# A rotary embedding's sin multiplication moved from VectorE to GpSimd, with six rotation buffers in place of three

## The reference, cut to what matters

```python
def _rotate_half(x):
    x1, x2 = (x[..., :R // 2], x[..., R // 2:])      # R = 64
    return jnp.concatenate([-x2, x1], axis=-1)

def _apply_rope(x, cos, sin):
    return x * c + _rotate_half(x) * s

kv_d = _lin(x, Wkv_d, bkv_d); q_d = _lin(x, Wq_d, bq_d)
k1 = _lin(kv_d, Wk_u, bk_u); kr = _apply_rope(_lin(x, Wrk, brk), cos, sin)
q1 = _lin(q_d, Wq_u, bq_u);  qr = _apply_rope(_lin(q_d, Wrq, brq), cos, sin)
k = jnp.concatenate([k1, kr], axis=-1); q = jnp.concatenate([q1, qr], axis=-1)
attn = softmax(q @ k / sqrt(D)); out = attn @ v; x = x + layernorm(out @ Wo + bo)
# then 16 experts, top 4 of them weighted, and a last layer norm
```

## Time and profile before

| what | us |
|---|---|
| runs shown | 8006.28 and 8179.35, median 8092.81 |
| the profiled execution, its own time | 8001.64 |
| its span on the slowest core (core 5) | 8000.1 |
| TensorE busy over the span | 6745.4 (84%) |
| VectorE busy over the span | 3149.2 (39%) |
| GpSimd busy over the span | 305.4 (4%) |

### The profile page before, as it was taken

One profiled execution on the slowest core, in us unless ns is written; L12 is line 12 of the kernel. 1 busy time (PEld: TensorE's weight loads), 2 busy tenths in 40 slices (PEclk: granted clock), 3 DMA queues, 4 the chain that ended last, 5 costly groups with the idle time before them and its releaser, 6 DMA issues.

```text
span 8000.1 us, 84460 instructions; the slowest of 8 cores (7974.1 to 8000.1 us)
## 1 busy us (share of the span) xinstructions
PE 6745.4 (84%) x31216; PEld 3081.5 (39%) x31216; DVE 3149.2 (39%) x5145; ACT 764.0 (10%) x1123; POOL 305.4 (4%) x563
## 2 busy tenths in 40 slices
PE   5444366666467999999999999999999999999995
PEld 2212122223243444444444444444444444444443
DVE  4333333334365343433434334343433434334344
ACT  2000033323010000000000000000000000000000
POOL 0111000000000000000000000000000000000000
PEclk9666566666677999999999999999999999999997
DMA  5111100000424333334334333334434334433334
GB/s 117 29 34 31 35 16 9 12 12 10 107 85 85 74 74 74 77 71 79 72 73 81 74 76 74 74 74 74 78 71 79 74 72 78 77 75 74 74 74 137
DMA packets 126286, 533.56 MB, mean 67 GB/s; under 512 B 34481, under 2 KB 59314, under 8 KB 67778
## 3 DMA queue, kind: packets, MB, share of 16 engines
q0 software_dynamic: 93184, 433.20, 29.2%
q1 hardware_dynamic: 32706, 94.96, 3.3%
HBM read 908.76 MB, written 37.75 MB: 118 GB/s over the span
## 4 chain that ended last, share of the span: by engine, by line
PE 77%; DVE 11%; DMA 6%; issue 4%; ACT 1%; DVEq 0%; another core or an unknown queue 0%; SPq 0%; ACTq 0%; POOL 0%; POOLq 0%
PE psum L1075 23%; PE psum L1030 22%; PE psum L1036 22%; DMA rotb<-krs 4%; PE psum L634 2%; PE psum L693 2%; DVE probsT L678 2%; PE psum L672 1%; PE psum L619 1%; DVE krs L462 1%; PE psum L425 1%; PE psum L891 1%; DVE stat L644 1%; DVE stat L829 1%; DVE stat L378 1%
## 5 line engine op out<-in xcount | busy, mean ns | idle before, releaser
L1030 PE MATMUL psum<-tT,w1sl 128*128 128x512 bf16 x8192 | 1854.7, 380 | 0.0
L1036 PE MATMUL psum<-tT,w1sl 128*128 128x512 bf16 x8192 | 1852.0, 380 | 0.0
L1075 PE MATMUL psum<-act_e,w2sl 128*128 128x512 bf16 x8192 | 1800.9, 384 | 50.5 <-DVE act_e L1059 50.5
L1075 PEld LDWEIGHTS psum<-act_e,w2sl 128*128 128x128 bf16 x8192 | 807.3, 99 | 1044.2 <-issue 98.7
L1030 PEld LDWEIGHTS psum<-tT,w1sl 128*128 128x128 bf16 x8192 | 800.4, 98 | 978.1 <-issue 16.4
L1036 PEld LDWEIGHTS psum<-tT,w1sl 128*128 128x128 bf16 x8192 | 801.1, 98 | 967.0
L1080 DVE TENSOR_TENSOR delta<-psum,delta 128x512 f32<-128x512 f32 x512 | 354.2, 692 | 1462.9 <-PE psum L1075 1462.9
L1045 DVE TENSOR_SCALAR ufs<-psum,b1sb 128x512 f32<-128x512 f32 x512 | 384.5, 751 | 1382.9 <-PE psum L1036 1382.9
L1054 ACT ACTIVATE sfs<-afs 128x512 f32<-128x512 f32 x512 | 322.2, 629 | 4971.2 <-DVE afs L1041 4971.1
L1041 DVE TENSOR_SCALAR afs<-psum,b1sb 128x512 f32<-128x512 f32 x512 | 384.4, 751 | 330.0 <-PE psum L1030 330.0
L1057 DVE TENSOR_TENSOR sfs<-sfs,ufs 128x512 f32<-128x512 f32 x512 | 354.6, 692 | 54.8 <-DVE ufs L1050 1.8
(11 more groups left out here) (129 smaller groups left out, 2896.8 us busy)
## 6 DMA issues: line engine op xcount, KB each, us to landing
w1sl<-w1s POOLq DMA_DIRECT2D x256, 1024.0 KB, 9.2
w2sl<-w2s POOLq DMA_DIRECT2D x128, 1024.0 KB, 7.9
xw<-xk SPq DMA_DIRECT2D x16, 1024.0 KB, 4.9
wo<-wo POOLq DMA_DIRECT2D x4, 2048.0 KB, 62.0
x1b<-xk SPq DMA_DIRECT2D x8, 1024.0 KB, 6.9
x_scr<-x1b SPq DMA_DIRECT2D x8, 1024.0 KB, 3.9
xn_scr<-xn1b SPq DMA_DIRECT2D x8, 1024.0 KB, 4.7
x1r<-x_scr SPq DMA_DIRECT2D x8, 1024.0 KB, 6.3
```

Of the source, the lines that this page charges most:

```text
L1030: bld.op("pe", lambda e, slA=slA, kc=kc, part=part, tc=tc, bkA=bkA: e.matmul(bank(bkA), w1sl[slA][:, kc * 256 + part * 128: kc * 256 + par ...
L1036: bld.op("pe", lambda e, slB=slB, kc=kc, part=part, tc=tc, bkB=bkB: e.matmul(bank(bkB), w1sl[slB][:, kc * 256 + part * 128: kc * 256 + par ...
L1075: bld.op("pe", lambda e, js=js, kc=kc, part=part, tc=tc, bk=bk: e.matmul(bank(bk), w2sl[js % 2][:, kc * 256 + part * 128: kc * 256 + part ...
```

## The change

The sin multiplication in `rope_a` is issued on GpSimd in place of VectorE. `krs` and `rotb` become six buffers each in place of three, so each of a head's six tiles has its own; they move to other addresses, and the names under which the later stages wait for the old buffers follow. In the changed kernel the lines of this part stand four lower: cos is L468, sin L471, the adds L479 and L492, the swap DMAs L462 and L465, the bias add L458.

```diff
-    krs = [sb("krs0", [128, 512], BF16, SEG_E + 16 * KB),
-           sb("krs1", [128, 512], BF16, SEG_D + 24 * KB),
-           sb("krs2", [128, 512], BF16, SEG_D + 28 * KB)]
...
+    krs = [sb(f"krs{i}", [128, 512], BF16, SEG_D + 24 * KB + i * KB) for i in range(6)]
+    rotb = [sb(f"rotb{i}", [128, 512], BF16, SEG_E + 8 * KB + i * KB) for i in range(6)]
...
-        bld.op("dve", lambda e, tc=tc, rb_=rb_, ro=ro: e.tensor_mul(
+        bld.op("pool", lambda e, tc=tc, rb_=rb_, ro=ro: e.tensor_mul(
             rb_[ro:ro + 64, :], rb_[ro:ro + 64, :], sink[ro:ro + 64, tc * 512:(tc + 1) * 512]),
             reads=(rr_, "sink"), writes=(rr_,))
...
-            rpA = gtile[0] % 3
+            rpA = gtile[0] % 6
...
-    for rn in ("krs1", "rotb1", "krs2", "rotb2"):
+    for rn in [f"krs{i}" for i in range(6)] + [f"rotb{i}" for i in range(6)]:
         for nn in ("probsT", "probs0", "probs1", "bvub"):
             bld.retire([rn], nn)
```

More of the change, by code:

```diff
@@ L323, in build_program @@
     sink = sb("sinkb", [128, SF], BF16, SEG_E + 4 * KB)
-    krs = [sb("krs0", [128, 512], BF16, SEG_E + 16 * KB),
-           sb("krs1", [128, 512], BF16, SEG_D + 24 * KB),
-           sb("krs2", [128, 512], BF16, SEG_D + 28 * KB)]
-    rotb = [sb("rotb0", [128, 512], BF16, SEG_E + 18 * KB),
-            sb("rotb1", [128, 512], BF16, SEG_D + 26 * KB),
-            sb("rotb2", [128, 512], BF16, SEG_D + 30 * KB)]
+    krs = [sb(f"krs{i}", [128, 512], BF16, SEG_D + 24 * KB + i * KB) for i in range(6)]
+    rotb = [sb(f"rotb{i}", [128, 512], BF16, SEG_E + 8 * KB + i * KB) for i in range(6)]
     bkv_sb = sb("bkvs", [128, 4], F32, SEG_E + 20 * KB)
@@ L513, in build_program @@
             bkA = gtile[0] % 4
-            rpA = gtile[0] % 3
+            rpA = gtile[0] % 6
             gtile[0] += 1
             bkB = gtile[0] % 4
-            rpB = gtile[0] % 3
+            rpB = gtile[0] % 6
             gtile[0] += 1
@@ L558, in build_program @@
             bk = gtile[0] % 4
-            rp = gtile[0] % 3
+            rp = gtile[0] % 6
             gtile[0] += 1
@@ L765, in build_program @@
     normw_b = sb("normwb", [128, 2048], F32, SEG_D + 16 * KB)
-    for rn in ("probsT", "probs0", "probs1", "bvub", "krs1", "rotb1", "krs2", "rotb2"):
+    for rn in ("probsT", "probs0", "probs1", "bvub") + tuple(f"krs{i}" for i in range(6)):
         bld.retire([rn], "bob")
@@ L784, in build_program @@
     grow = sb("grow", [1, TOK], F32, SEG_E + 6 * KB)
-    for rn in ("cosk", "sink"):
+    for rn in ("cosk", "sink") + tuple(f"rotb{i}" for i in range(6)):
         for nn in ("GT", "GTp", "grow"):
```

## The result

The change makes the kernel 0.6% slower: the ratio is 1.0058 with a 95% interval of 1.004 to 1.0076, some 46 us. The profiled execution of the changed kernel spans 8050.7 us on its slowest core, against 8000.1. The median of the 11 runs is 8816.96 us, and of the 10 of the kernel before 8095.73, but in most of the changed kernel's runs the cores of a die ran at a lower clock, so the ratio compares the undisturbed ones, at 8051.67 to 8055.55 us after and 8001.76 to 8012.11 us before.

A forecast was written before the change was run, and what follows sets the result against it. The prediction took VectorE together with its swap DMAs to bound the stage of keys and queries. Its terms, -33 (sin) + 7 (SP's extra wait) + 43 (collision) = +17 us on 8001.64, gave 8019 us, range 7955 to 8140.

The forecast's parts named there:

- The ring: Stage of keys and queries: VectorE with its swap DMAs sets the length, 399.6 us waiting plus 252.98 work of 667.
- The cos keeps the wait: On VectorE the cos, not the sin, waits for the swap DMAs, so the 399.6 us of waiting stays.
- The sin's 0.34 us: On VectorE, removing each sin saves only the 0.34 us between starts, 96 x 0.34 = 33 us.
- rival 1: GpSimd reads while VectorE reads, without collision: -33 + 7 = -26, 7976 us; chance 0.29.
- The buffers at 0: Six krs and rotb buffers in place of three buy nothing and cost 0, as VectorE hardly waited for a buffer.
- The add's wait for GpSimd: VectorE's add of the tile before now waits for GpSimd's sin; a sin up to some 4 us is hidden.
- SP's second wait: Before the swap DMA SP also waits for GpSimd's sin of six tiles ago: 0.08 us, 90 times, +7 us.
- The collision: VectorE's add and GpSimd's sin of 0.69 us can't both read: +0.67 us on 64 L496 adds, +43 us.
- Rival 2: Full exclusion: each sin holds VectorE's add or cos for its whole length, +61 to +105 us, 8063 to 8107; chance 0.24.
- The sum by the Trainium skill: With a sin of 1.11 us the collision on VectorE's add would be 64 x 1.09 = +70 us, program 8045.
- Same, within 2%: Whole program: time changes by no more than about 2% (some 160 us) either way; chance 0.95.
- What I said would show it: On VectorE, cos start to add start: some 1.1 us in two thirds of tiles, against 0.34 to 0.44 without collision.

The follow-up runs named there:

- no_dma_in_turn: Everything on VectorE, cos writing its own buffer, a tile's two swap DMAs not waiting for each other, sin a tile later: 7652.03 us, against 8002.46 for the kernel before.
- add_in_wait: Changed kernel with the previous tile's add moved ahead of the cos: 7938.27 us with the sin on GpSimd, 7964.40 us with it on VectorE.
- six_buffers_only: Changed kernel with the sin multiplication back on VectorE, so only the six buffers are left of the change: 8002.02 us.
- three_buffers: Changed kernel with the sin on GpSimd, but the buffers taken in turn from three as before the change: 8049.36 us.

## Why the prediction was right or wrong

- *The ring*: right. VectorE with its DMAs set the length of the stage: what was put into or taken out of VectorE's turn came out in the time, whole or in the main, in every kernel here. no_dma_in_turn shows the size of the wait: without it, and with the sin a tile later, the stretch was 350 us shorter.
- *The cos keeps the wait*: right, 399.2 against 399.6 us.
- *The sin's 0.34 us*: right where nothing collides (0.33 in the tile at 527.58 above). Over the 96 tiles the pair of add_in_wait gave 26 us between the lowest times, which is the -33 + 7 of rival 1, and 18 on average over the cores.
- *The buffers at 0*: right (six_buffers_only, three_buffers).
- *The add's wait for GpSimd, hidden up to 4 us*: right; no wait in the profile.
- *SP's second wait, +7 us*: a gap longer by 0.06 us is there. The 8 cores make 4 to 6 us of it likely, from one execution of each kernel.
- *The collision, +43 us*: the step that failed, in its size. "I take 0.69" for the sin was wrong: it lasts 1.39 us beside VectorE, at my upper bound (1.38), and 1.15 to 1.20 alone. "The 32 L483 adds slip in before" was wrong too: 25 of the 32 were stretched, and their mean is 1236 ns. On the other side, I had put the sin behind the whole cos. It starts with it and loses only about 0.2 us, so an L492 add is 0.84 us longer and not 0.42 + 1.39 - 0.44 = 1.37. In sum VectorE of the slowest core spends 48 us more between cos and the following bias add over the 96 tiles, in place of 33 less: the collision cost 81 us there, and 76 on average over the 8 cores (43 more in place of 33 less), where my sum had 43.
- *Rival 2*, full exclusion, is nearest to what happened; it had 0.24. With its price of 61 to 105 us over all it was too dear by the overlap just named. The estimate of 1.11 us for the sin, from the 2.6 cycles an element that the Trainium skill gives ("GPSIMD Engine Reference", section "Performance versus the Vector engine"), was nearer than my row from another engine: 1.15 to 1.20 alone. The sum by the Trainium skill, 8045, is 7 us from the lowest run measured (8051.67), partly by luck: it left out the L483 adds and the overlap, which are of opposite sign.
- *Same, within 2%*: right. The sum of 8019 is 32 us below the profiled execution's span of 8050.7; the direction was right and the size a third. My range, 7955 to 8140, holds the profiled execution and not the median of the 11 runs (8816.96). Its upper end was a reach taken from two runs that differ by 2%, and I took that for all of the spread; the 11 runs spread by 14%, and no step of mine was about that. From rival 2's 8107 to 8140 is also nearer half of the way to the higher run shown than the third that I wrote.
- *What I said would show it*: I named a longer time from the start of the cos to the start of the add. The start stayed where it was, at 0.34 to 0.46 us in all tiles but the one with the long cos; the blocked time stands as busy time of the add itself.

## What to carry to other kernels

Before an elementwise instruction is moved from VectorE to GpSimd, look at what runs beside it at the moment that releases it: an operation on two SBUF tensors there is stretched until just behind the end of GpSimd's reading instruction, which here made the move cost 81 to save 33 us. And before an instruction is taken off a waiting engine, ask whether it is the one that waits: here the price stood on the cos, which overwrote what two DMAs were reading, and a second buffer, a second name and a sin one tile later were together worth 350 us, where the move of the sin was worth at best 26.

## What the runs showed of the hardware that I had not expected

- The exclusion shows as a longer instruction, not as idle time: 0.42 became 1.26 us (L492 add), 1.38 to 1.74 (L479 add), 1.37 (sin), 1.12 (cos, when GpSimd was first).
- The held instruction ends 0.27 to 0.30 us after GpSimd's (87 of 88 in the changed kernel), even where it started 0.14 to 0.27 us before it.
- It took a GpSimd instruction that reads: a copy with one input of 783 ns stretches VectorE's sin to 768 ns, a memset of 525 ns doesn't touch it.
- An add that starts only 0.34 us behind the cos is held as well as one at 0.45.
- TensorE's granted clock in the stage was 0.66 where it was busy 273.78 of 667 us, and 0.84 where it was busy 221.93 of 320, so a bound worked out at half the clock (3.4 us a tile) didn't come to hold.
